# The two routing exponentials on ScalarE, issued at the end of the turn that makes the scores instead of in the next one

## The chip, the cores and the metric

The kernel is one program on one core of a Trainium2 chip. The metric is the device time of one execution in microseconds (us), as the median of several runs. The engines are named as the profile names them: PE is TensorE's matmuls and PEld its weight loads, DVE is VectorE, ACT is ScalarE, POOL is GpSimd, and SP is SyncE, which here only issues DMAs.

## What is computed

Two layers over x (16 batches of 256 tokens, width 256), float32 throughout, matrix products in split high and low parts. Each layer is attention followed by a feed-forward part:

```python
x = x + L0_xattn(ctx, layernorm(x))      # stage A of the kernel
x = x + L0_ffn(layernorm(x))             # gelu, low-rank extra weights per batch
x = x + L1_xattn(layernorm(x), ctx, ctx)
x = x + L1_ffn(layernorm(x))             # 8 experts, routed
```

The change is in the last line's routing, of which this is the part that matters:

```python
inh = sigmoid(x @ Wr / temperature)
in_zone = (inh >= GOLDEN_LOWER) & (inh <= GOLDEN_UPPER)
dist = abs(inh - GOLDEN_CENTER)
w = exp(-dist / 0.1) * in_zone
fb = exp(-dist / 0.3)
...                     # top 2 of fb where w is empty, then both normalised
out = einsum('bte,betd->btd', weights, e_out)   # e_out of all 8 experts
```

## The kernel before

Stage A (names with a_) runs the first attention and writes x1 to HBM. Stage B (names with b_), from about 1150 us on, does the rest: one turn for each batch. Turn t holds the dense part of batch t (the gelu layer, the second attention, the routing scores) and, woven into it, the experts of batch t - 1. There are 17 turns, t = 0 to 16: turn 0 has no experts, turns 1 to 14 are the hardware loop, turn 15 has no next batch, and turn 16 has experts only. A turn has eight slots, e = 0 to 7. Each engine has its own in-order list of instructions, written out by hand slot by slot, and the engines meet at counting semaphores only.

In slot e of a turn, PE makes gate and up of expert e + 1 (`gate_up`, into b_ps_g and b_ps_u) and then the down product of expert e (`down`, into b_ps_d), with the dense pieces, called fills, between: H are the gelu layer's columns, Y its second product, K, V, Q, S, T, O the attention, A, B, C the transposes behind a layer norm, R the routing scores. `gate_up` of expert 0 of batch t stands in slot 7 of turn t, `gate_up` of expert 1 in slot 0 of turn t + 1.

ACT turns a gate into `silu` (L998, b_act_e), and copies the hidden product into its high part (`hidden_high`, L1002, b_heh). DVE multiplies by up (`hidden`, L1167), makes the low part (`hidden_low`, L1171, b_hel) and adds the weighted down product to acc (`weigh`, L1184). `weights_high` (L990) and `weights_low` (L1147) split pieces of the gelu layer's weights, which POOL has summed with a low-rank term (`low_rank`, L923 and L933) in b_stage.

The scores of batch t are fill R of slot 6: ACT takes a tanh (L1040), DVE makes b_dist from it (L1233 to L1240) and signals `dist_ready`. The two exponentials are `routing_exps`. DVE's `routing` (L1265 to L1303) makes the weights b_wts from them in 14 small steps, in four parts within slot 0 of the next turn. In that slot DVE's order is: `hidden` of expert 1, routing part 0, `hidden_low` of expert 1, part 1, low part of fill H0, part 2, low part of H1, part 3 and b_wts, one `weights_low`, `weigh` of expert 0. What comes after depends on it so:

```python
def weigh(i, e):
    dve.wait_ge(down_full, i * E + e + 1)
    if e == 0:
        dve.wait_ge(wts_ready, i + 1)
...
def down(i, e):
    pe.wait_ge(he_lo, i * E + e + 1)
    pe.wait_ge(acc_ready, i * E + e + 1)     # weigh of expert e - 1
```

An ACT function that is not in the set of tables at hand needs an ACT_TABLE_LOAD; the build puts it ahead of the function, where ACT's order asks for it. Silu and tanh share one set here, gelu has another, exp a third; the plain copy is in all.

Of the kernel before, what the change touches and what calls it, by code (L numbers as in the profile page):

```python
# [632 lines left out]
def ffn_attention_experts(nc, x1, ctxT, out, lora, W1T, b1, W2T, b2, scale, WqT, bq, WkT, bk, WvT, bv, Wg, Wu, Wd, Wr,  # L633
# [5 lines left out]
    E = Wg.shape[0]  # L639
# [10 lines left out]
    def slot(e, nb, nn):  # L650
        if e == 0 and nb:
            return [("H", n) for n in range(HC // 2)], []
        if e == 1 and nb:
            return [], [("Y",)]
        if e == 2 and nb:
            return [("K",), ("V",)], [("B",)]
        if e == 3 and nb:
            return [("Q",)], [("S",)]
        if e == 4 and nb:
            return [("T",)] + ([("A",)] if nn else []), [("O",)]  # L660
        if e == 5 and nb:
            return [], [("C",)]
        if e == 6 and nb:
            return [], [("R",)]
        return [], []

    def turn_fills(nb, nn):
        return [f for e in range(E) for part in slot(e, nb, nn) for f in part]
# [19 lines left out]
    with ctx:  # L688
# [74 lines left out]
        def sections_of(eng, body):  # L763


            first = Fills(names_all, 1, 1, start)
            body(first, 0, False, True, True)
            with eng.Fori(1, B - 1) as t:
                body(Fills(names_all, 1, 1, first, F, FH, t), t, True, True, True)
            loop = Fills(names_all, 0, 0, None)  # L770
            last = Fills(turn_fills(True, False), 1 + F * (B - 1), 1 + FH * (B - 1), loop)
            body(last, B - 1, True, True, False)
            body(Fills([], 0, 0, last), B, True, False, False)
# [27 lines left out]
        def warm_pieces(e):  # L801
            first = 3 + sum(WARM_SLOTS[:e])
            return range(first, first + sum(WARM_SLOTS[e:e + 1]))
# [169 lines left out]
        def _(act):  # L973
            def warm_high(k):
                act.wait_ge(weights.loaded[k // 3], 3 * 16)
                raw, dh, _ = warm_weight(k)
                nc.scalar.activation(dh, raw, ACT.Copy, scale=QSCALE if k == 0 else 1.0).then_inc(warm_hi, 1)
# [5 lines left out]
            def weights_high(n, k):  # L983

                act.wait_ge(stage_sum, n * CHUNKS + k + 1)
                if k < NL:
                    dst = w1h[:, k // 2, k % 2 * 2 * D:(k % 2 + 1) * 2 * D]
                else:
                    dst = w2h[:, 2 * (k - NL):2 * (k - NL) + 2, :].rearrange("p c d -> p (c d)")
                nc.scalar.activation(dst, stage[:, k % STAGES, :], ACT.Copy).then_inc(stage_hi, 1)  # L990

            def context_high(t):
                act.wait_ge(ct_in, t * 16 + 16)
                nc.scalar.activation(cth[:], ct_raw[:], ACT.Copy).then_inc(ct_hi, 1)

            def silu(i, e):
                act.wait_ge(gate_full, i * E + e + 1)
                nc.scalar.activation(act_e[:, e % 2, :], ps_g[:], ACT.Silu).then_inc(silu_done, 1)  # L998

            def hidden_high(i, e):  # L1000
                act.wait_ge(he_ready, i * E + e + 1)
                nc.scalar.activation(heh[:, e % 2].rearrange("p c s -> p (c s)"), act_e[:, e % 2, :], ACT.Copy)\  # L1002
                    .then_inc(he_hi, 1)
# [45 lines left out]
            def routing_exps(t):  # L1049
                act.wait_ge(dist_ready, t + 1)  # L1050
                nc.scalar.activation(wz[:], dist[:], ACT.Exp, scale=-1.0 / 0.1).then_inc(exps_ready, 1)
                nc.scalar.activation(fb[:], dist[:], ACT.Exp, scale=-1.0 / 0.3).then_inc(exps_ready, 1)
# [9 lines left out]
            def turn(fills, t, experts, nb, nn):  # L1062
                i = 0

                def highs(names):
                    nonlocal i
                    for _ in names:
                        high(fills, i, t, experts)
                        i += 1

                def steps_of(e, part):
                    for k in PIECES.get((e, part), ()) if nn else ():
                        weights_high(t + 1, k)
                    for k in (LATE if experts else LATE_FIRST).get((e, part), ()) if nb else ():
                        weights_high(t, k)

                for e in range(E):
                    steps_of(e, 0)
                    if e + 1 < E and experts:
                        silu(t - 1, e + 1)  # L1080
                    elif e + 1 == E and nb:
                        silu(t, 0)
                    before, after = slot(e, nb, nn)
                    if e == 0 and experts:
                        routing_exps(t - 1)
                        hidden_high(t - 1, 1)
                    highs(before[:2])
                    if not experts:
                        for k in warm_pieces(e):
                            warm_high(k)  # L1090
                    if e == 1 and nb:
                        context_high(t)
                    if 0 < e < E - 1 and experts:
                        hidden_high(t - 1, e + 1)
                    elif e + 1 == E and nb:
                        hidden_high(t, 0)
                    steps_of(e, 1)
                    highs(before[2:])
                    highs(after)
                    steps_of(e, 2)  # L1100
            sections_of(act, turn)

        @block.vector
# [474 lines left out]
```

## Time and profile before

| | |
|---|---|
| time, 3 runs | 2188.25 us median, 2186.59 to 2188.69 |
| the profiled execution: span | 2184.7 us |
| PE busy | 91% |
| DVE busy | 71% |
| ACT busy | 52% |
| POOL busy | 29% |
| mean granted clock of TensorE | 0.967 |

The profiled execution is known by its span from the first to the last instruction, 2184.7 us; the median of the runs is 3.55 us above it, a difference of 0.2% that holds what lies around the span and the scatter of the runs. Busy shares are means over stages with different limits, so they don't say what a wait in one slot is worth. A clock of 1.00 is TensorE at 2.4 GHz, 0.5 is 1.2 GHz.

### The profile page before, as it was taken

To read this page: it belongs to the slowest core of one execution; us is meant where nothing else is said; L and a number is where in the kernel's file an instruction comes from. 1 tells how busy PE (TensorE), PEld (TensorE's weight loads), DVE (VectorE), ACT (ScalarE), POOL (GpSimd) and SP (SyncE) were. 2 spreads that over 40 slices of the span, in tenths; PEclk is the share of its full clock that TensorE was granted. 3 is DMA by queue.
4 is the path that set the end of the run, shared out by engine and by line. 5 is a ranking of instruction groups with operands and counts; after the bars stand their busy time and mean duration, and the time that the engine had idled before them with its cause. 6 is when DMAs were issued, how large, how long until landed. Compare 5 with 4: busy or idle time off the path is not lost.

```text
span 2184.7 us, 43173 instructions
## 1 busy us (share of the span) xinstructions
PE 1993.4 (91%) x14080; PEld 1855.1 (85%) x14080; DVE 1540.9 (71%) x3506; ACT 1133.3 (52%) x2307; POOL 636.3 (29%) x802
## 2 busy tenths in 40 slices
PE   6999999999999999999458889889889988889988
PEld 5888888888888888888348889888889888889888
DVE  6777767676767777776466787777776777786765
ACT  5565555565555556555254554455454455454442
POOL 1222222222222222221223444234444234443220
PEclk9999999999999999999768999999999999999999
DMA  5000000000000000000231222111222111212100
GB/s 176 11 20 19 19 19 10 10 19 19 19 19 19 10 10 19 19 10 10 78 101 35 73 66 69 53 63 38 72 63 72 53 63 38 72 63 72 53 20 11
DMA packets 86022, 92.16 MB, mean 42 GB/s; under 512 B 7008, under 2 KB 77024, under 8 KB 85984
## 3 DMA queue, kind: packets, MB, share of 16 engines
q1 hardware_dynamic: 82720, 88.53, 13.1%
q10 hardware_dynamic: 3264, 3.15, 0.4%
q8 instruction: 21, 0.34, 0.1%
q14 instruction: 17, 0.14, 0.0%
HBM read 83.00 MB, written 8.65 MB: 42 GB/s over the span
## 4 chain that ended last, share of the span: by engine, by line
PE 17%; DVE 16%; issue 9%; DMA 3%; ACT 3%; DVEq 1%; SPq 1%; POOL 0%; ACTq 0%; POOLq 0%
DMA b_even<-lora_rows 3%; PE b_ring L1401 3%; PE b_ring L1402 3%; PE b_ring L1403 3%; DVE b_acc L1184 3%; DVE b_act_e L1167 1%; ACT b_heh L1002 1%; PE b_ps_d L1401 1%; DVE b_w1l L1147 1%; PE b_ps_d L1403 1%; PE b_ps_d L1402 1%; PE b_ps_g L1401 1%; PE b_ps_g L1403 1%; PE b_ps_g L1402 1%; PE b_ps_u L1401 1%
## 5 line engine op out<-in xcount | busy, mean ns | idle before, releaser
L236 POOL TENSOR_SCALAR a_pr<-a_pr,a_rinv 128x512 f32<-128x512 f32 x256 | 182.4, 726 | 489.0 <-DVE a_rinv L441 486.1
L317 ACT ACTIVATE a_pr<-a_sim,a_nmax 128x512 f32<-128x512 f32 x256 | 174.3, 688 | 201.5 <-DVE a_nmax L431 201.5
L1401 PE MATMUL b_ps_d<-b_weh,b_heh 128*128 128x256 f32 x512 | 154.2, 301 | 62.2 <-DVE b_acc L1184 62.2
L998 ACT ACTIVATE b_act_e<-b_ps_g 128x512 f32<-128x512 f32 x128 | 76.3, 596 | 187.5 <-PE b_ps_g L1403 187.0
L499 PE MATMUL a_ring<-a_kvh,a_weights_low 128*128 128x512 f32 (+1 forms) x512 | 172.0, 336 | 0.0
L408 DVE SCALAR_TENSOR_TENSOR a_ktl<-a_ring,a_bkv_s,a_kth 128x512 fp32r<-128x512 f32 x128 | 95.2, 744 | 102.0 <-ACT a_kth L296 102.0
L422 DVE TENSOR_TENSOR a_ptl<-a_ring,a_pth 128x512 fp32r<-128x512 f32 x256 | 163.7, 681 | 1.2
L431 DVE TENSOR_REDUCE a_nmax<-a_sim 128x1 f32<-128x512 f32 x256 | 163.5, 679 | 0.3 <-PE a_sim L499 0.3
L1401 PEld LDWEIGHTS b_ps_d<-b_weh,b_heh 128*128 128x128 f32 x512 | 103.4, 202 | 65.2 <-issue 63.3
L898 POOL TENSOR_SCALAR b_rows<-b_mv 128x2 f32<-128x2 f32 x48 | 9.6, 199 | 508.9 <-DVE b_mv L1116 508.9
L1002 ACT ACTIVATE b_heh<-b_act_e 128x512 fp32r<-128x512 f32 x128 | 80.9, 632 | 144.4 <-DVE b_act_e L1167 144.4
L1403 PE MATMUL b_ps_d<-b_weh,b_hel 128*128 128x256 f32 x512 | 152.0, 297 | 0.0
L418 DVE TENSOR_TENSOR a_vl<-a_ring,a_vh 128x512 fp32r<-128x512 f32 x128 | 88.5, 692 | 89.3 <-ACT a_vh L304 89.3
L933 POOL TENSOR_TENSOR b_stage<-b_stage,b_ln 128x512 f32<-128x512 f32 x96 | 136.7, 1424 | 45.2 <-DVE b_stage L1136 30.9
L1401 PE MATMUL b_ps_g<-b_xch,b_weh 128*128 128x256 f32 x512 | 148.6, 290 | 0.0
L497 PE MATMUL a_ring<-a_pth,a_vh 128*128 128x256 f32 x512 | 144.5, 282 | 3.5 <-DVE a_ptl L422 3.4
L1402 PE MATMUL b_ps_g<-b_xcl,b_weh 128*128 128x256 f32 x512 | 144.9, 283 | 0.0
L499 PE MATMUL a_ring<-a_pth,a_vl 128*128 128x256 f32 x512 | 144.8, 283 | 0.0
L498 PE MATMUL a_ring<-a_ptl,a_vh 128*128 128x256 f32 x512 | 144.8, 283 | 0.0
L1401 PE MATMUL b_ps_u<-b_xch,b_weh 128*128 128x256 f32 x512 | 144.5, 282 | 0.0
L1402 PE MATMUL b_ps_u<-b_xcl,b_weh 128*128 128x256 f32 x512 | 144.2, 282 | 0.0
L307 ACT ACTIVATE a_pth<-a_ring 128x512 fp32r<-128x512 f32 x256 | 139.2, 602 | 0.0
(224 smaller groups left out, 7345.0 us busy)
## 6 DMA issues: line engine op xcount, KB each, us to landing
b_stage<-in_W1T SPq DMA_DIRECT2D x64, 256.0 KB, 2.9
b_even<-lora_rows SPq DMA_DIRECT2D x32, 512.0 KB, 5.9
b_stage<-in_W2T SPq DMA_DIRECT2D x64, 256.0 KB, 2.7
a_c_in<-in_ctx_in SPq DMA_DIRECT2D x16, 256.0 KB, 2.8
a_x_in<-in_x SPq DMA_DIRECT2D x16, 256.0 KB, 3.0
a_x_res<-in_x SPq DMA_DIRECT2D x16, 256.0 KB, 2.8
x_between<-a_x_out SPq DMA_DIRECT2D x16, 256.0 KB, 2.2
b_x_s<-x_between SPq DMA_DIRECT2D x16, 256.0 KB, 2.6
```

What stands on the lines that cost most here:

```text
L236: nc.gpsimd.tensor_scalar(pr[:, h % 2, t, :], pr[:, h % 2, t, :], rinv[:, h % 2, t:t + 1], 1.0, ALU.mult, ALU.mult).then_inc(prob_ready, 1)
L307: nc.scalar.activation(pth[:, :, name[2] * P:(name[2] + 1) * P], bank[:].rearrange("p (k q) -> p k q", k=KT), ACT.Copy).then_inc(ring_hi, 1)
L317: nc.scalar.activation(pr[:, h % 2, t, :], sim[t][:], ACT.Exp, bias=nmax[:, h % 2, t:t + 1], accum_out=rsum[:, h % 2, t:t + 1]).then_inc(e ...
L422: nc.vector.tensor_tensor(ptl[:, :, cols], bank[:].rearrange("p (k q) -> p k q", k=KT), f32(pth[:, :, cols]), ALU.subtract).then_inc(ring_ ...
L431: nc.vector.tensor_reduce(nmax[:, h % 2, t:t + 1], sim[t][:], AX.X, ALU.max, negate=True)\
L497: nc.tensor.matmul(out, lh, rh, start=(n == 0), stop=False)
L498: nc.tensor.matmul(out, lh, rl, start=False, stop=False)
L499: last = nc.tensor.matmul(out, ll, rh, start=False, stop=(n == len(parts) - 1))
L933: nc.gpsimd.tensor_tensor(stage[:, k % STAGES, :], stage[:, k % STAGES, :], ln[:].rearrange("p c d -> p (c d)"), ALU.add).then_inc(stage_s ...
L1401: nc.tensor.matmul(out, lh, rh, start=(n == 0), stop=False)
L1402: nc.tensor.matmul(out, lh, rl, start=False, stop=False)
L1403: last = nc.tensor.matmul(out, ll, rh, start=False, stop=(n == len(parts) - 1))
```

## The change

`routing_exps` is called in another place of ACT's list: no more in slot 0 of the turn of the experts, behind `silu` of expert 1, but at the very end of slot 7 of the turn before, for the same batch. Nothing is computed otherwise, and no other engine's list is touched.

```diff
@@ -1082,7 +1082,6 @@
                         silu(t, 0)
                     before, after = slot(e, nb, nn)
                     if e == 0 and experts:
-                        routing_exps(t - 1)
                         hidden_high(t - 1, 1)
                     highs(before[:2])
                     if not experts:
@@ -1098,6 +1097,8 @@
                     highs(before[2:])
                     highs(after)
                     steps_of(e, 2)
+                    if e + 1 == E and nb:
+                        routing_exps(t)
             sections_of(act, turn)
```

ACT's list before, where a turn of the loop ends (L768 is the loop's branch) and slot 0 of the next begins; b_act_e is silu, b_wz and b_fb are the two exponentials, b_heh is `hidden_high`:

```order
L1002 ACTIVATE b_heh<-b_act_e 128x512
L985 REGISTER_ALU
L990 ACTIVATE b_w1h<-b_stage 128x512
L768 REGISTER_ALU
L768 COMPARE_AND_BRANCH
L990 ACTIVATE b_w2h<-b_stage 128x512
L998 ACTIVATE b_act_e<-b_ps_g 128x512
L1051 ACT_TABLE_LOAD
L1051 ACTIVATE b_wz<-b_dist 128x16
L1052 ACTIVATE b_fb<-b_dist 128x16
L1002 ACTIVATE b_heh<-b_act_e 128x512
L1027 ACT_TABLE_LOAD
```

The same place in ACT's list of the change:

```order
L990 ACTIVATE b_w1h<-b_stage 128x512
L1051 ACT_TABLE_LOAD
L1051 ACTIVATE b_wz<-b_dist 128x16
L1052 ACTIVATE b_fb<-b_dist 128x16
L768 REGISTER_ALU
L768 COMPARE_AND_BRANCH
L990 ACTIVATE b_w2h<-b_stage 128x512
L998 ACT_TABLE_LOAD
L998 ACTIVATE b_act_e<-b_ps_g 128x512
L1002 ACTIVATE b_heh<-b_act_e 128x512
L1027 ACT_TABLE_LOAD
```

The exponentials and their table load stand ahead of a piece of weights and of silu of expert 1, and silu now has a table load of its own: one more in each of these turns.

The piece of the difference at the end of turn 15 and in turn 16, which has no weights to split and no gelu:

```order
 L998 ACTIVATE b_act_e<-b_ps_g 128x512
 L1002 ACTIVATE b_heh<-b_act_e 128x512
-L998 ACTIVATE b_act_e<-b_ps_g 128x512
 L1051 ACT_TABLE_LOAD
 L1051 ACTIVATE b_wz<-b_dist 128x16
 L1052 ACTIVATE b_fb<-b_dist 128x16
-L1002 ACTIVATE b_heh<-b_act_e 128x512
-L998 ACT_TABLE_LOAD
+L998 ACT_TABLE_LOAD
+L998 ACTIVATE b_act_e<-b_ps_g 128x512
+L1002 ACTIVATE b_heh<-b_act_e 128x512
 L998 ACTIVATE b_act_e<-b_ps_g 128x512
```

Here the number of table loads stays; the load for silu moves from behind to ahead of silu of expert 1.

## Rows read from the trace of the kernel before

**Rows 1.** The waits of PE, 1160 us to the end: total us, times, longest.

```profile
PE b_ps_d L1401 <- DVE b_acc L1184: 62.2, 17, 4.2
```

**Rows 2.** Timeline of PE, 1371.6 to 1372: start, us, instruction [idle before].

```profile
1371.67 0.36 PE L1401 MATMUL b_ps_d<-b_weh,b_heh 128*128 128x256 f32 x1 [3.79 <-DVE b_acc L1184]
```

**Rows 3.** Timeline of DVE, 1354 to 1372.

```profile
1358.25 0.67 DVE L1147 TENSOR_TENSOR b_w2l<-b_stage,b_w2h 128x512 fp32r<-128x512 f32 x1
1358.85 0.67 DVE L1167 TENSOR_TENSOR b_act_e<-b_act_e,b_ps_u 128x512 f32<-128x512 f32 x1
1359.44 0.67 DVE L1265 TENSOR_TENSOR b_wz<-b_wz,b_near 128x16 f32<-128x16 f32 x1
...
1364.23 0.71 DVE L1277 TENSOR_TENSOR b_fb<-b_fb,b_mask 128x16 f32<-128x16 f32 x1
...
1366.09 1.26 DVE L1280 TENSOR_SCALAR b_rows<-b_rows 128x2 f32<-128x2 f32 x1
...
1369.94 0.17 DVE L1303 TENSOR_TENSOR b_wts<-b_wz,b_rows 128x16 f32<-128x16 f32 x1
```

**Rows 4.** Timeline of ACT, 1354.5 to 1361.6.

```profile
1355.06 0.61 ACT L990 ACTIVATE b_w1h<-b_stage 128x512 fp32r<-128x512 f32 x1
1355.88 0.63 ACT L990 ACTIVATE b_w2h<-b_stage 128x512 fp32r<-128x512 f32 x1 [0.21 <-POOL b_stage L933]
1356.42 0.58 ACT L998 ACTIVATE b_act_e<-b_ps_g 128x512 f32<-128x512 f32 x1
1357.02 1.28 ACT L1051 ACT_TABLE_LOAD   x1
1358.31 0.22 ACT L1051 ACTIVATE b_wz<-b_dist 128x16 f32<-128x16 f32 x1
1358.44 0.20 ACT L1052 ACTIVATE b_fb<-b_dist 128x16 f32<-128x16 f32 x1
```

**Rows 5.** Timeline of ACT, 1399 to 1400.5.

```profile
1399.90 0.60 ACT L998 ACTIVATE b_act_e<-b_ps_g 128x512 f32<-128x512 f32 x1
```

**Rows 6.** Timeline of DVE, 1399 to 1401.6.

```profile
1400.53 0.69 DVE L1167 TENSOR_TENSOR b_act_e<-b_act_e,b_ps_u 128x512 f32<-128x512 f32 x1 [1.11 <-ACT b_act_e L998]
```

**Rows 7.** Timeline of POOL, 1354 to 1368.

```profile
1358.30 1.78 POOL L933 TENSOR_TENSOR b_stage<-b_stage,b_ln 128x512 f32<-128x512 f32 x1 [0.18 <-POOL b_ln L923]
1360.65 1.42 POOL L923 TENSOR_TENSOR b_ln<-b_even,b_odd 128x256 f32<-128x256 f32 x2 [0.56 <-POOL b_stage L933]
1362.25 1.29 POOL L933 TENSOR_TENSOR b_stage<-b_stage,b_ln 128x512 f32<-128x512 f32 x1 [0.18 <-POOL b_ln L923]
1363.72 1.90 POOL L923 TENSOR_TENSOR b_ln<-b_even,b_odd 128x256 f32<-128x256 f32 x2 [0.18 <-POOL b_stage L933]
1365.70 1.62 POOL L933 TENSOR_TENSOR b_stage<-b_stage,b_ln 128x512 f32<-128x512 f32 x1
```

**Rows 8.** Timeline of DVE, 2085.3 to 2093.2 (slot 0 of turn 15).

```profile
2087.09 1.26 DVE L1277 TENSOR_TENSOR b_fb<-b_fb,b_mask 128x16 f32<-128x16 f32 x1
...
2092.02 0.17 DVE L1303 TENSOR_TENSOR b_wts<-b_wz,b_rows 128x16 f32<-128x16 f32 x1
```

**Rows 9.** Timeline of POOL, 2081 to 2090.

```profile
2086.62 1.70 POOL L933 TENSOR_TENSOR b_stage<-b_stage,b_ln 128x512 f32<-128x512 f32 x1
```

**Rows 10.** Timeline of ACT, 2140 to 2147.6 (end of turn 15, turn 16).

```profile
2140.66 0.63 ACT L1002 ACTIVATE b_heh<-b_act_e 128x512 fp32r<-128x512 f32 x1 [1.61 <-DVE b_act_e L1167]
2142.72 0.60 ACT L998 ACTIVATE b_act_e<-b_ps_g 128x512 f32<-128x512 f32 x1 [1.43 <-PE b_ps_g L1403]
```

**Rows 11.** Timeline of DVE, 2143 to 2145.6.

```profile
2144.21 0.69 DVE L1167 TENSOR_TENSOR b_act_e<-b_act_e,b_ps_u 128x512 f32<-128x512 f32 x1 [1.41 <-PE b_ps_u L1403]
2145.09 0.18 DVE L1265 TENSOR_TENSOR b_wz<-b_wz,b_near 128x16 f32<-128x16 f32 x1 [0.20 <-ACT b_fb L1052]
```

**Rows 12.** Windows behind PE's wait: us, busy (count) of PE, PEld, DVE, ACT, POOL, clock, DMA.

```profile
1370.00:1380.00 10.00, 7.95 (x54) 7.68 (x55) 6.60 (x13) 4.79 (x8) 0.00 (x0) 0.83 0.10 26
...
1632.00:1642.00 10.00, 8.36 (x50) 8.39 (x51) 6.58 (x13) 4.77 (x8) 0.00 (x0) 0.66 0.08 26
```

## The prediction

> **What bounds the kernel now.** PE is busy for 91% of the span, so I read first what PE waits for. In the table of waits one entry stands out in stage B: `down` of expert 1 waits for `weigh` of expert 0, 62.2 us in all, the longest 4.2 us [rows 1]. The timeline of PE at one such place has 3.79 us of idle time [rows 2]. There is one such wait in each of the 16 turns with experts, in slot 0 or, in turn 16, at its head. So whatever delays `weigh` of expert 0 delays PE, one for one, and what hastens it is a gain of up to 3.79 us a turn.
>
> Behind `weigh` stands DVE's list. In its timeline DVE goes from `weights_low` (1358.25) to `hidden` of expert 1 (1358.85), the first routing step (1359.44) and on to b_wts at 1369.94 with hardly a gap [rows 3]. The second exponential has ended at 1358.44 + 0.20 = 1358.64 [rows 4]. DVE comes to the routing at 1359.44, 0.80 us later. So in the loop the exponentials are not waited for: DVE's own list sets the pace. Only in turn 16 does the first step wait for them, 0.20 us [rows 11].
>
> The third reader is POOL, whose sums run beside this until 1365.70 + 1.62 = 1367.32 [rows 7]. Several DVE steps on 16 or fewer columns, which elsewhere take 0.16 to 0.18 us, take far longer here, and end when a POOL instruction ends: the first routing step at 1360.11 (POOL 1360.08), L1280 at 1367.35 (POOL 1367.32) [rows 3, 7]. DVE and POOL shut each other out for whole instructions, so a delay on DVE need not come out at the same size.
>
> **The change, part by part.** *What it takes away.* Two exponentials and a table load leave the place between silu of expert 1 and `hidden_high` of expert 1. They ended at 1358.64, and `hidden_high` can't start before `hidden` at 1358.85 has run, so nothing was waiting: 0. In turn 16 the wait of 0.20 us goes.
>
> *What it adds ahead of silu of expert 1.* I rebuild ACT's list from its rows. The last piece of weights of the turn ends at 1355.06 + 0.61 = 1355.67. Then a table load of 1.28, to 1356.97 with the 0.02 that stands ahead of the load in the rows. Exponentials: the first starts 0.01 after its load, and the second ends 0.33 after the first starts (1358.31 to 1358.64), so to 1357.31. b_dist is long there, it came in slot 6. Then the piece b_w2h; it starts some 0.02 before the end of the second exponential and takes 0.63: to 1357.92. Then the new table load of silu, to 1359.22, and silu, 0.60, to 1359.82. Before, silu ended at 1356.42 + 0.58 = 1357.00, with 1.85 us to spare until DVE came for it at 1358.85. Now it is late. How soon DVE starts once silu has ended is to be seen in another slot: silu ends at 1400.50, `hidden` starts at 1400.53 [rows 5, 6]. So `hidden` moves from 1358.85 to 1359.86, by 1.0 us. That is the stall the change makes: 2.82 us more on ACT (1359.82 - 1357.00) less 1.85 us of slack, plus 0.03.
>
> Queued ahead on DVE, `weights_low` of the same piece starts at 1358.25 and needs b_w2h, now at 1357.92 instead of 1356.51: still in time by 0.3 us. The stage buffers that it frees, their DMAs on SP and POOL's sums are then not late. PE needs silu of expert 1 only for the gate of expert 2 and `down` 0 not at all; both were covered before and stay so. Queued behind `hidden` on DVE is the whole routing, then `weigh` of expert 0, for which PE waits.
>
> What a load itself costs is plain here: L1051's load starts at 1357.02, takes 1.28 and the exponential starts at 1358.31 [rows 4]. The Trainium skill (ScalarE: Activation LUTs, What ACT_TABLE_LOAD costs) adds a drain of about 1.38 us to each load, 2.66 us together. By that silu would be later by another 2 x 1.38 us, and 15 turns would cost some 41 us more. The trace disagrees, the next instruction starts 0.01 us behind the load, so the sum goes by 1.28.
>
> *What POOL makes of 1.0 us.* I carry the delay through the two lists. `hidden` reads PSUM and is not held up. The first routing step comes at 1360.46 instead of 1359.44: it finds POOL between two instructions (1360.08 to 1360.65) and takes 0.16, not 0.67, so half a microsecond comes back. L1270, the first step on the maxima, then comes about 1.1 us later, at 1361.6, and meets POOL's products, which end at 1360.65 + 1.42 = 1362.07, so 1362.10. L1272 comes 0.3 behind its predecessor's start, at about 1362.3, 0.07 after POOL's sum has begun (1362.25 to 1363.54): ends 1363.57. L1275 meets the products from 1363.72 on; its two steps and `hidden_low` (0.68) end at about 1365.8. POOL's last sum, waiting since 1365.3, goes then, 1.29 on its own, to about 1367.0. L1277 is queued behind it and ends at 1367.04. The same pattern is in the trace once, in turn 15: L1277 is held for 1.26 us, to 2088.35, by POOL's sum that ends at 2088.32, and b_wts starts at 2092.02, 3.70 after that end [rows 8, 9]. So here b_wts comes at 1367.0 + 3.7 = 1370.7, against 1369.94: **0.8 us** later. The bounds are 0 (POOL's last end holds L1280 in both cases) and 1.0 (no give and take), and I take 0.8 for each of the 15 turns 1 to 15: 12.0 us.
>
> *Turn 16.* No POOL. ACT is idle between `hidden_high` of expert 0 (ends 2141.29) and silu (2142.72) [rows 10]. Load, exponentials and load fill it: 2141.29 + 1.30 + 0.33 + 1.30 = 2144.22, silu to 2144.82. `hidden` starts at 2144.85, not 2144.21; the first routing step follows 0.60 later (from 1358.85 to 1359.44 in rows 3) at 2145.45 instead of 2145.09: 0.4 us.
>
> *The clock.* Behind PE's wait the granted clock falls to 1.2 GHz for a while. I read 16 windows of 10 us, each from about the end of the wait: 11 have a mean clock of 0.83, as the first row shows, 5 have 0.66, as the second [rows 12]. The difference is 0.17 x 10 = 1.7 us of PE's time. The idle time grows from 3.79 to about 4.6 us, and the longest wait of all, 4.2 us [rows 1], is followed by one of the five. Bounds: none more, or all of the other 11, 11 x 1.7 = 19 us. I take two or three more: 4 us.
>
> **The sum.** 12.0 + 0.4 + 4 = 16.4 us on a span of 2184.7, 2201.1. The median of the runs is 3.55 us above that execution's span: **2204.6 us**, +0.75%. A measurement of this kernel tells about 0.2% (4.4 us) from no change.
>
> **The rivals.**
> - *Full delay.* POOL's pattern shifts with DVE, or the order of L1272 and POOL's sum comes out so that more is held: 1.0 to 1.3 a turn, and half of the other gaps get the long stretch of slow clock (9 us): 15 x 1.15 + 0.4 + 9 = 27, 2215. For it: L1272 loses by only 0.07 us. Against: POOL's end comes earlier by my walk, not later.
> - *Swallowed.* POOL's last sum holds the chain at 1367.3 as before: if L1277 gets in ahead of that sum, L1280 is what waits for it, as now, and the 1.0 us of stall is given back by shorter holds. 15 x 0 + 0.4 and no clock, 2188.7. Against it: in the rows `hidden_low` is followed by exactly this race now (POOL's products at 1363.72, L1277 at 1364.23), and POOL wins, L1277 being held to 1364.94. The Trainium skill (SBUF — State Buffer, Who interferes with whom) says that whoever issues first has the shared port for its whole instruction; that speaks for POOL in this race too, and leaves the 0.8.
> - *Faster, the other side.* That the exponentials come early frees ACT between silu and `hidden_high`, and the routing finds its inputs. A gain needs the routing to have waited for them. If the hold of DVE's first routing step (0.67 us) was such a wait in disguise, its 0.51 over 0.16 comes back in 15 turns and the silu must arrive in time as well, that is the added 2.82 us must be under 1.85: at most 15 x 0.51 + 0.2 = 7.9, 2180.4. It decides only if the second table load doesn't occur or lies in idle time, and ACT has none there (0.21 and then none).
> - *Nothing of the stall,* since silu's load is fetched while ACT waits: 2188. ACT does not wait there in the loop.
>
> **How the numbers follow.** Forecast (0.5 to 0.9 a turn, clock 0 to 8) 66%; full delay and more 16%; swallowed, wholly or to under 4 us, 12%; faster 3%; nothing 3%. The forecast's own span is 15 x 0.5 + 0.4 = 7.9 to 15 x 0.9 + 0.4 + 8 = 21.9 above 2188.25; the range reaches into full delay on the one side and to 4.8 us above on the other, halfway to swallowed: 2193 to 2214. Faster by over 0.2% 0.03, within 0.2% 0.11, slower 0.86.
>
> **What would show it.** In the profile after: L998 has 15 more table loads; in slot 0 DVE idles about 0.9 us before L1167, released by ACT's silu; b_wts comes about 0.8 us later counted from the same piece of PE's work; PE's wait for b_acc grows from 62 to about 74 us; L1280 is short and L1277 long; and more windows at 0.66. The prediction is wrong if that wait does not grow, if `hidden` starts on time, or if the clock takes most of the difference.

## The result and the profile after

The change made the kernel slower: 2197.1 us median (2196.8 to 2198.21) against 2188.35 us for the kernel before in the same set, +8.75 us, ratio 1.0044 with a 95% interval of 1.0029 to 1.0058. The forecast was +16.4 us, 2204.6, with a range of 2193 to 2214: the time lies in the range, in its lower part, at little more than half of the forecast difference. The profiled executions have spans of 2184.7 before and 2195.2 after, 10.5 us apart. In every execution the device time is some 1.8 us above the span, so the profiled one of before ran 1.8 us below its kernel's median and the one after sits on its own (2197.0): 10.5 and 8.75 are the same difference, to what two single executions can tell.

The waits of PE after, from 1160 us to the end (total us, times, longest), then the page's group of `down`, then two rows of the answer on `silu`'s line, its table loads and who waited for silu, and the same two rows of before. Line numbers behind the change are one higher:

```profile
PE b_ps_d L1402 <- DVE b_acc L1185: 72.0, 17, 4.6
```

```profile
L1402 PE MATMUL b_ps_d<-b_weh,b_heh 128*128 128x256 f32 x512 | 153.4, 300 | 72.0 <-DVE b_acc L1185 72.0
```

```profile
L998 ACT ACT_TABLE_LOAD  x47: 1283/1283/1283, 1154.7 to 2154.0; - x47
  DVE b_act_e L1168: 32.1, 31
```

```profile
L998 ACT ACT_TABLE_LOAD  x32: 1283/1283/1283, 1153.8 to 2145.6; - x32
  DVE b_act_e L1167: 17.3, 15
```

The wait for b_acc, 62.2 us in [rows 1], is 72.0 us now, 9.8 us more, and so it stands in the page's group. Silu's line has 47 table loads where it had 32, and DVE now waits for silu 31 times, not 15: in each of the turns 1 to 16 once more. From PE's wait in turn 1 (it ends at 1175.42 before, at 1176.16 after) to its last wait (2179.59 and 2190.03) the two executions differ by 9.7 us, so from there on the wait is their whole difference.

ACT's timeline around the start of turn 4, to be held against [rows 4]. The anchor here is the last piece of weights of the turn, 1356.64 now and 1355.06 there, so the same place of the work stands 1.58 us later in this trace:

```profile
1356.64 0.62 ACT L990 ACTIVATE b_w1h<-b_stage 128x512 fp32r<-128x512 f32 x1
1357.27 1.28 ACT L1051 ACT_TABLE_LOAD   x1
...
1358.80 0.61 ACT L990 ACTIVATE b_w2h<-b_stage 128x512 fp32r<-128x512 f32 x1
1359.43 1.28 ACT L998 ACT_TABLE_LOAD   x1
1360.72 0.60 ACT L998 ACTIVATE b_act_e<-b_ps_g 128x512 f32<-128x512 f32 x1
```

Silu ends at 1361.32, which is 1359.74 in the times of before; the prediction had 1359.82. Nothing stands between a load and its neighbours but 0.01 to 0.02 us. DVE and POOL in the same place, to be held against [rows 3] and [rows 7]:

```profile
1359.82 0.68 DVE L1148 TENSOR_TENSOR b_w2l<-b_stage,b_w2h 128x512 fp32r<-128x512 f32 x1
1361.35 0.69 DVE L1168 TENSOR_TENSOR b_act_e<-b_act_e,b_ps_u 128x512 f32<-128x512 f32 x1 [0.86 <-ACT b_act_e L998]
1361.96 0.17 DVE L1266 TENSOR_TENSOR b_wz<-b_wz,b_near 128x16 f32<-128x16 f32 x1
...
1363.88 1.25 DVE L1273 TENSOR_SCALAR b_rows<-b_rows 128x2 f32<-128x2 f32 x1
...
1367.28 1.26 DVE L1278 TENSOR_TENSOR b_fb<-b_fb,b_mask 128x16 f32<-128x16 f32 x1
...
1369.49 0.16 DVE L1281 TENSOR_SCALAR b_rows<-b_rows 128x2 f32<-128x2 f32 x1
...
1372.24 0.17 DVE L1304 TENSOR_TENSOR b_wts<-b_wz,b_rows 128x16 f32<-128x16 f32 x1
```

```profile
1359.88 1.77 POOL L933 TENSOR_TENSOR b_stage<-b_stage,b_ln 128x512 f32<-128x512 f32 x1 [0.18 <-POOL b_ln L923]
1362.22 1.42 POOL L923 TENSOR_TENSOR b_ln<-b_even,b_odd 128x256 f32<-128x256 f32 x2 [0.56 <-POOL b_stage L933]
1363.82 1.29 POOL L933 TENSOR_TENSOR b_stage<-b_stage,b_ln 128x512 f32<-128x512 f32 x1 [0.18 <-POOL b_ln L923]
1365.29 1.44 POOL L923 TENSOR_TENSOR b_ln<-b_even,b_odd 128x256 f32<-128x256 f32 x2 [0.18 <-POOL b_stage L933]
1366.81 1.69 POOL L933 TENSOR_TENSOR b_stage<-b_stage,b_ln 128x512 f32<-128x512 f32 x1
```

```profile
1373.97 0.55 PE L1402 MATMUL b_ps_d<-b_weh,b_heh 128*128 128x256 f32 x1 [4.52 <-DVE b_acc L1185]
```

DVE idles 0.86 us for silu. The first routing step then takes 0.17 us, not 0.67: it finds POOL between two instructions (1361.65 to 1362.22). The step on the row sums (L1273) is held for 1.25 us, and ends at 1365.13 with POOL's sum (1365.11). L1278, L1277 before, is held for 1.26 us, until 1368.54 (POOL 1368.50), and L1281, L1280 before, is free, 0.16 instead of 1.26. b_wts starts at 1372.24, that is 1370.66 in the times of before, against 1369.94 in [rows 3]: 0.72 us later. PE's idle time is 4.52 against 3.79 in [rows 2].

All of turns 2 to 14 look like this one, with idle times of 4.49 to 4.57 us. Three turns differ. In turn 1 and in turn 15 PE's wait has not grown: in turn 15 it is 4.18 us, where the longest of before was that turn's 4.2 [rows 1]. POOL's holds there gave the whole delay back. For turn 15 the rows say how: its L1277 was held by POOL's last sum in the kernel before already, for 1.26 us [rows 8, 9], and L1278 is held for 1.26 us now, so the end of that sum sets b_wts in both:

```profile
2099.11 1.26 DVE L1278 TENSOR_TENSOR b_fb<-b_fb,b_mask 128x16 f32<-128x16 f32 x1
```

In turn 16 the wait has grown by 0.4 us: `hidden` waits for silu, and the first step comes that much later than it did behind its own wait for the exponentials [rows 11]. 13 x 0.72 + 0.4 = 9.8 us, which is the growth of the wait.

The granted clock made no difference between these two executions in stage B (their means over everything, 0.967 and 0.969, differ by stage A, 0.97 and 0.98). Of the 16 windows of 10 us behind the waits, 9 have a mean of 0.83, 6 have 0.66 and one, turn 1's, has 1.00:

```profile
1174.00:1184.00 10.00, 7.19 (x58) 7.01 (x59) 6.84 (x14) 5.20 (x9) 0.00 (x0) 1.00 0.11 27
1241.00:1251.00 10.00, 8.58 (x58) 8.47 (x59) 6.36 (x12) 4.49 (x7) 0.00 (x0) 0.83 0.10 26
...
1372.00:1382.00 10.00, 8.03 (x47) 8.06 (x48) 6.76 (x14) 5.02 (x8) 0.00 (x0) 0.66 0.08 26
```

By the price of [rows 12] that is 9 x 1.7 + 6 x 3.4 = 35.7 us of PE's time against 11 x 1.7 + 5 x 3.4 = 35.7 before: one more long stretch, one short one less.

This price is too high, and that changes what the clock can explain below. It takes all time at the low clock to be time in which PE works at half its speed. The length of a turn, from one b_wts to the next, shows what arrives. In the kernel before, the turns from turn 2 to turn 14 last 66.2 us on average where the stretch behind the wait is a long one (a window of 0.66; 3 turns) and 65.5 us where it is a short one (0.83; 9 turns); after the change 67.0 us (5 turns) and 66.0 us (7 turns). In these two traces a long stretch costs 0.7 to 0.9 us more than a short one, not 1.7.

### The profile page after: what moved, and what is told of

The parts are those of the page before. It is cut to its first block, busy times and chain, and to the rows that moved or that the text cites. A ratio compares the mean times of both kernels' runs of the same rounds, so it can differ in the third digit from the quotient of the medians.

```text
span 2195.2 us, 43188 instructions
## 1 busy us (share of the span) xinstructions
PE 1992.6 (91%) x14080; PEld 1854.0 (84%) x14080; DVE 1537.3 (70%) x3506; ACT 1151.9 (52%) x2322; POOL 629.3 (29%) x802
## 4 chain that ended last, share of the span: by engine, by line
PE 17%; DVE 15%; issue 9%; ACT 5%; DMA 3%; DVEq 1%; POOL 0%; SPq 0%; ACTq 0%; POOLq 0%
PE b_ring L1402 3%; DMA b_even<-lora_rows 3%; PE b_ring L1404 3%; PE b_ring L1403 3%; DVE b_acc L1185 2%; DVE b_act_e L1168 1%; ACT L998 1%; PE b_ps_d L1402 1%; PE b_ps_d L1404 1%; PE b_ps_d L1403 1%; DVE b_w1l L1148 1%; ACT b_heh L1002 1%; PE b_ps_g L1402 1%; PE b_ps_g L1404 1%; PE b_ps_g L1403 1%
## 5 line engine op out<-in xcount | busy, mean ns | idle before, releaser
L1168 DVE TENSOR_TENSOR b_act_e<-b_act_e,b_ps_u 128x512 f32<-128x512 f32 x128 | 87.3, 682 | 79.3 <-PE b_ps_u L1404 47.2
```

Of the source, the lines that this page charges most:

```text
L1168: nc.vector.tensor_tensor(act_e[:, e % 2, :], act_e[:, e % 2, :], ps_u[:], ALU.mult).then_inc(he_ready, 1)
```

## The experiments

Theory: silu of expert 1 comes too late behind a table load, the exponentials and a second load, and the mutual holds of DVE and POOL decide what of it reaches PE. The rivals are that an added table load, or the place, costs by itself, and that the clock makes the difference. Each ratio is to the kernel before, timed in the same set: 2186.39 us for e0, e1, e2 and e5, and 2186.22 us on another chip for e3, e4, e6 and e7.

**The change once more, as a control (e0_after).** No edit.

> The changed kernel once more, as the control of this set. Theory (silu of expert 1 comes 0.94 us too late, of which DVE's list passes on 0.72 us a turn): as measured first, +8 to +10 us, PE's wait for b_acc 72 us in all, that is 4.5 us in each of turns 2 to 14. Rival (most of the difference is the slow clock, which falls otherwise from run to run): the difference to the kernel before moves by more than 3 us, and the number of long stretches of slow clock behind the waits is no longer near 6 of 16.

Measured: 2195.7 us (2193.74 to 2200.99) against 2186.39, ratio 1.0053 (1.0041 to 1.0065), that is +9.3 us, as the theory said. The wait for b_acc is 72.0 us again and turns 2 to 14 have 4.49 to 4.54 us each. The windows behind the waits have 7 of the long slow stretches (0.66) and 9 short ones, against 6 and 9 in the first execution. So the wait is the same to the tenth. By the price of 1.7 us the clock costs 9 x 1.7 + 7 x 3.4 = 39.1 us here, 3.4 more, and yet this execution has the shorter span, 2193.2 against 2195.2 us; PE's wait for b_ln, 9.4 us there, is 6.6 us here. The single executions of this set spread over 7 us. The rival of the clock isn't borne out: the difference to the kernel before is the same and so is the wait.

**The exponentials further ahead still (e1_exps_behind_silu0).**

```diff
                     elif e + 1 == E and nb:
                         silu(t, 0)
+                        routing_exps(t)
...
                     if e == 0 and experts:
-                        routing_exps(t - 1)
                         hidden_high(t - 1, 1)
```

> The exponentials move further ahead still, right behind silu of expert 0 in slot 7, where ACT idles for about 3 us before hidden_high of expert 0. As many table loads as in the change. Theory (the loss is the table load and exponentials between the last piece of weights and silu of expert 1): only silu's own load, 1.30 us, is left there, under the 1.85 us of slack, so hidden of expert 1 is on time: 2188, 0 to -1 us against before, PE's wait 3.8 us a turn. Rival (an added table load costs its time wherever it stands, or early exponentials as such cost): +8 us or more.

Measured: 2183.46 us (2179.73 to 2189.62), ratio 0.9992 (0.9984 to 1.0001); no difference. ACT's timeline at the end of turn 3 and the start of turn 4:

```profile
1349.38 0.60 ACT L998 ACTIVATE b_act_e<-b_ps_g 128x512 f32<-128x512 f32 x1 [0.65 <-PE b_ps_g L1403]
1350.00 1.28 ACT L1051 ACT_TABLE_LOAD   x1
1351.87 0.22 ACT L1051 ACTIVATE b_wz<-b_dist 128x16 f32<-128x16 f32 x1 [0.59 <-DVE b_dist L1240]
...
1355.09 1.28 ACT L998 ACT_TABLE_LOAD   x1
1356.39 0.60 ACT L998 ACTIVATE b_act_e<-b_ps_g 128x512 f32<-128x512 f32 x1
```

DVE's `hidden` of that turn:

```profile
1357.40 0.67 DVE L1167 TENSOR_TENSOR b_act_e<-b_act_e,b_ps_u 128x512 f32<-128x512 f32 x1
```

That is as the theory said, within the noise. The load and the exponentials fit into ACT's idle time ahead of `hidden_high` of expert 0, and even wait there for b_dist, 0.59 us. Silu ends at 1356.99, 0.41 us before DVE asks for it. There are as many table loads as in the change, and no loss: the added load is free where ACT idles. The waits for b_acc are 62.1 us, as before.

**The place of the change without the loads (e2_copies_no_loads).**

```diff
-nc.scalar.activation(wz[:], dist[:], ACT.Exp, scale=-1.0 / 0.1).then_inc(exps_ready, 1)
-nc.scalar.activation(fb[:], dist[:], ACT.Exp, scale=-1.0 / 0.3).then_inc(exps_ready, 1)
+nc.scalar.activation(wz[:], dist[:], ACT.Copy, scale=-1.0 / 0.1).then_inc(exps_ready, 1)
+nc.scalar.activation(fb[:], dist[:], ACT.Copy, scale=-1.0 / 0.3).then_inc(exps_ready, 1)
```

> The place of the change, but both exponentials are plain copies with a scale, which need no table load: this leaves the exponentials of the routing out (the routing weights are other numbers, all instructions on the other engines are the same). Theory: 0.33 us more ahead of silu of expert 1 and no load, inside the slack of 1.85 us: 2188, within 1 us of before. Rival (the place as such costs, by the wait for b_dist or by the two instructions at the loop's branch): +8 us.

Measured: 2185.24 us (2182.07 to 2189.33), ratio 0.9999 (0.999 to 1.0007). The waits for b_acc are 61.8 us in all and 3.76 to 3.83 in turns 2 to 14. The place as such costs nothing.

**The same place, plain copies instead of the loads (e6_copies_and_padding).** As e2, and behind the second copy:

```diff
+for n in range(4):
+    nc.scalar.activation(hh[:, 2 * n:2 * n + 2, :], wqkvh[:, 0], ACT.Copy)
+for n in range(2):
+    nc.scalar.activation(gel[0][:, n * D:(n + 1) * D], wqkvh[:, 0, 0, :], ACT.Copy)
```

> As e2_copies_no_loads (the exponentials of the routing left out, copies in their place, no table load), with six plain copies more behind them, 2.8 us on ACT into tiles that nobody reads then. Silu of expert 1 ends about as late as in the change. Theory (the loss is lateness of silu alone, whatever fills the time): hidden of expert 1 about 0.9 us later, PE's wait 4.5 us in turns 2 to 14, +7 to +10 us, as the change. Rival (the table loads cost by themselves): like e2_copies_no_loads, 2185 to 2188, with waits of 3.8 us.

Measured: 2197.42 us (2195.11 to 2202.8), ratio 1.0053 (1.0038 to 1.0068), as the change. Its waits, and DVE's timeline at the start of turn 4:

```profile
PE b_ps_d L1406 <- DVE b_acc L1189: 72.1, 17, 4.5
```

```profile
1364.23 1.03 DVE L1152 TENSOR_TENSOR b_w2l<-b_stage,b_w2h 128x512 fp32r<-128x512 f32 x1 [0.81 <-ACT b_w2h L990]
1365.19 0.67 DVE L1172 TENSOR_TENSOR b_act_e<-b_act_e,b_ps_u 128x512 f32<-128x512 f32 x1
...
1367.00 1.21 DVE L1275 TENSOR_SCALAR b_rows<-b_rows 128x2 f32<-128x2 f32 x1 [0.16 <-DVE b_top_at L1274]
```

A table load isn't needed for the loss; time on ACT does it, though not quite by the way expected. The copies come ahead of the piece b_w2h, and here DVE waits for that piece (0.81 us) before it comes to `hidden`; silu, behind the piece, is there by then. So `hidden` is 1.25 us late and not 0.9. Counted from the end of PE's up product of expert 1 (1356.48 in the kernel before, so 1358.85 - 1356.48 = 2.37 for `hidden`), `hidden` starts at 3.62 us against 2.37 in the kernel before and 3.30 in the change, but b_wts at 14.16 against 13.46 and 14.19. So a delay of 1.25 us and one of 0.93 us both come out as 0.7. What reaches b_wts is set by where POOL's instructions end, not by the size of the delay.

**The same pair without POOL beside it (e3_before_quiet_pool, e4_after_quiet_pool).** Both kernels with this edit in `low_rank`:

```diff
+if k >= CHUNKS - 3:
+    last = nc.gpsimd.memset(ln[:, 0, 0:8], 0.0)
-for c in range(DC):
+for c in range(DC) if k < CHUNKS - 3 else ():
...
+w = 2 * D if k < CHUNKS - 3 else 8
-nc.gpsimd.tensor_tensor(stage[:, k % STAGES, :], stage[:, k % STAGES, :], ...
+nc.gpsimd.tensor_tensor(stage[:, k % STAGES, 0:w], stage[:, k % STAGES, 0:w], ...
```

> The kernel before, with POOL's work on weight pieces 5, 6 and 7 cut to 8 columns: this leaves most of the low-rank term of these pieces out. All waits and the lists of the other engines stay. It is the pair of e4_after_quiet_pool and read against it. Theory (DVE's and POOL's holds pass on only a part of the delay): DVE's routing steps all take 0.16 to 0.23 us, hidden of expert 1 comes about 0.5 us earlier than in the kernel before, b_wts some 7 us after hidden instead of 11.1, and PE's wait of 3.8 us all but goes: below 2120 us.

> The changed kernel with the same cut on POOL; it leaves the same out. Silu of expert 1 then comes at its time of the change, and the distance between the two kernels of this pair in hidden of expert 1 is 1.4 to 1.5 us. Theory (what was given back, 0.94 us on hidden and only 0.72 on b_wts, was given back by POOL's holds): without POOL there is nothing to give back, b_wts is later by the whole of hidden's delay, within 0.1 us, and the pair differs by 10 us or more. Rival (DVE's list has a fixed slack of 0.2 us behind hidden, whatever POOL does): b_wts is later by 0.2 us less than hidden, or more if gelu on ACT is what DVE waits for.

Measured: 2110.04 us (ratio 0.9654, 0.9639 to 0.967) and 2133.89 us (0.9763, 0.9746 to 0.978), 23.9 us apart. DVE in turn 4 without the change, then with it:

```profile
1341.23 0.68 DVE L1170 TENSOR_TENSOR b_act_e<-b_act_e,b_ps_u 128x512 f32<-128x512 f32 x1
1341.82 0.17 DVE L1268 TENSOR_TENSOR b_wz<-b_wz,b_near 128x16 f32<-128x16 f32 x1
...
1348.79 0.18 DVE L1306 TENSOR_TENSOR b_wts<-b_wz,b_rows 128x16 f32<-128x16 f32 x1
```

```profile
1349.90 0.69 DVE L1171 TENSOR_TENSOR b_act_e<-b_act_e,b_ps_u 128x512 f32<-128x512 f32 x1 [1.22 <-ACT b_act_e L1001]
1350.51 0.17 DVE L1269 TENSOR_TENSOR b_wz<-b_wz,b_near 128x16 f32<-128x16 f32 x1
...
1357.47 0.17 DVE L1307 TENSOR_TENSOR b_wts<-b_wz,b_rows 128x16 f32<-128x16 f32 x1
```

From `hidden` to b_wts there are 7.56 us without and 7.57 us with the change, where they were 11.09 and 10.89 with POOL at work. From the end of up, `hidden` goes from 1.84 to 3.30 and b_wts from 9.40 to 10.87: 1.46 and 1.47 us. The whole delay arrives, nothing is given back, so the 0.2 us that were given back in the real kernel were POOL's. In turns 2 to 14 PE's wait for b_acc is at most 0.29 us without the change and 1.70 to 1.73 us with it; in all it is 9.8 and 32.5 us, which is nearly all of the difference of the two. The rival of a fixed slack is out.

**The early place used (e5_early_and_first_steps).** As e1, and on DVE:

```diff
-first, last = ((0, 5), (5, 7), (7, 11), (11, ROUTE))[part]
+first, last = ((2, 5), (5, 7), (7, 11), (11, ROUTE), (0, 2))[part]
...
                     elif e + 1 == E and nb:
+                        routing(t, 4)
                         hidden_low(t, 0)
```

with the wait for the exponentials in part 4.

> As e1_exps_behind_silu0, and the first two of the 14 routing steps on DVE move from slot 0 to slot 7 of the turn before, between hidden and hidden_low of expert 0, where DVE idles 0.70 us for ACT. Theory: with the exponentials done at about 1353.7 the two steps (1.0 us of instructions, 0.7 of it in the idle time) leave the list ahead of weigh, so b_wts comes 0.6 to 1.2 us earlier a turn and PE's wait falls to about 3.0: -9 us, 2179 (0.996). Rival (POOL holds the steps up in their new place, or hands the hold on to the next step): nothing gained, 2188, with the waits at 3.8.

Measured: 2169.4 us (2168.14 to 2173.03), ratio 0.9926 (0.9914 to 0.9939): faster than both kernels, and by 17 us, not 9. Its waits, PE's timeline in turn 4, and the window behind that wait:

```profile
PE b_ps_d L1402 <- DVE b_acc L1184: 51.3, 17, 3.4
PE b_ring L1402 <- DVE b_w1l L1147: 16.3, 14, 1.2
```

```profile
1371.51 0.36 PE L1402 MATMUL b_ps_d<-b_weh,b_heh 128*128 128x256 f32 x1 [3.09 <-DVE b_acc L1184]
```

```profile
1371.00:1381.00 10.00, 9.45 (x65) 9.18 (x66) 5.80 (x11) 3.58 (x6) 0.00 (x0) 0.83 0.08 26
```

The wait for b_acc falls by 62.2 - 51.3 = 10.9 us, a little more than the expected 9. The clock, which the expectation left out, has improved as well: 1 window of 16 has 0.66, 14 have 0.83 and one 1.00. By the price of 1.7 us that is 14 x 1.7 + 3.4 = 27.2 against 35.7 us, 8.5 us less, and 10.9 + 8.5 = 19.4 us. The profiled executions differ by 2184.7 - 2171.2 = 13.5 us, so of these 8.5 us some 2.6 arrive. The medians differ by 17 us; the profiled execution is the slowest of its five.

**More steps early (e7_first_five_steps).** As e5, with the parts `((5, 5), (5, 7), (7, 11), (11, ROUTE), (0, 5))`.

> As e5_early_and_first_steps, with the first five routing steps in slot 7 instead of two. Theory (the idle time of DVE there is 0.70 us and is used up): three more steps, 2 to 3 us with POOL's holds, push weights_low ahead of fill H0, so PE's wait for b_w1l grows by about what its wait for b_acc falls: the sum of the two about as in e5_early_and_first_steps, 2166 to 2176. Rival (more steps early are more gain): another 1.5 us a turn, 2150.

Measured: 2187.61 us (2186.56 to 2190.57), ratio 1.0012 (1.0004 to 1.0021).

```profile
PE b_ring L1402 <- DVE b_w1l L1147: 61.0, 14, 4.5
...
PE b_ps_d L1402 <- DVE b_acc L1184: 5.9, 8, 1.7
```

```profile
1757.00:1767.00 10.00, 8.50 (x49) 8.51 (x50) 8.71 (x17) 6.31 (x12) 6.56 (x6) 0.66 0.27 79
```

The wait has moved nearly whole, from b_acc to b_w1l, and the sum of the two, 66.9 us, is that of e5 (67.6), as the theory said. The time is neither what the theory said (2166 to 2176) nor the rival's 2150: it is 18 us more than in e5, and 13.6 us between the two profiled executions (2171.2 and 2184.8). Of these, 6.5 us are waits of PE: all its waits in stage B are 90.9 us in e5 and 97.4 here, mostly by the wait for b_w2l, 0.6 us there and 7.1 here. One wait of 4.5 us has taken the place of two of 1.2 and 3.1, and 9 of the 16 windows behind it have 0.66 to 0.74 where e5 has one. That the clock took the rest isn't shown: between b_wts of turn 2 and of turn 14, turns with a long stretch last 65.8 us here (8 turns) and those with a short one 65.9 (4 turns), where all of e5's, with short ones, last 64.9. What the other 7 us are stays open.

## Why the prediction was right, step by step

- *PE waits for `weigh` of expert 0, one for one.* Right. The wait is 9.8 us longer; the span is 10.5 us longer, 9.7 of it behind PE's wait in turn 1.
- *Nothing waits for the exponentials, so taking them away gains 0.* Right; e1 has them 5 us earlier at no gain. Their wait in turn 16 went, 0.2 us, as said.
- *ACT's list: 2.82 us more, 1.85 us of slack, `hidden` 1.0 us later.* Measured 0.93 from the same point of PE's work. The piece b_w2h starts at once behind the exponentials, with 0.09 us of overlap where I had 0.02. That lateness is the cause, and not the load or the place, is shown by e1, e2 and e6 together.
- *POOL gives back 0.2 us: 0.8 a turn.* Right in its mechanism and almost in its size: L1277 held by the last sum, L1280 free, b_wts 3.7 us behind POOL's end, 0.72 us. It was applied to all of turns 1 to 15; in turns 1 and 15, where POOL runs at another phase, the delay was given back whole. For turn 15 that could be read ahead: I took its rows as the pattern of what the change would do, so it had that pattern already and nothing was to come on top. 13 x 0.72 + 0.4 = 9.8 instead of 15 x 0.8 + 0.4 = 12.4: this term was 2.6 us too large.
- *The clock, 4 us.* This is the term that was most mis-sized. The direction was right: the profiles have 1 long stretch in 16 at a wait of 3.1 us (e5), 5, 3 and 4 at 3.8 us (before, e1, e2), 6, 7 and 8 at 4.5 us (the change, e0, e6). That is three more on average, and I took two or three, but from one case, the longest wait. The profile of before, with 5, was the highest of its kind and that of after, with 6, the lowest, so between these two nothing came of it. The price of 1.7 us was wrong: a long stretch adds 0.7 to 0.9 us to its turn in these two traces. And the times leave little for it: the three kernels with waits of 4.5 us are 8.75, 9.3 and 11.2 us slower than the kernel before, and their waits are 9.8 to 9.9 us longer.
- *The scale.* The sum was put on top of a median that lay 1.8 us above the profiled execution's own time, and the difference of the medians was 8.75, not 10.5.
- *The sum.* The path was right and the size of the wait right to 2.6 us. The 16.4 us are nearly twice the 8.75 measured by these 2.6 us, the clock's 4 us and 1.8 us of scatter, less the 0.7 us that the spans differ beyond the wait. The time still fell into the range, 4 us above its lower end; the range was wide enough for that, and the point forecast was not close.
- *The rivals.* Full delay (27 us) would have needed POOL out of step with DVE. Swallowed came true in two turns of sixteen, in one of them because the pattern was there before. A gain by the exponentials being early didn't occur.

## What to carry to other kernels

An instruction that is moved ahead to where "nobody waits for it" is moved past its neighbours: ask which of them gets late, and count the slack of that one, here 1.85 us against 2.82. With function tables, a move can split two functions of one set and add a load; the load is free only in time in which the engine idles, and such a place, 3 us wide, lay a few instructions further ahead in the same slot (e1). An early result is worth something only once its consumer is moved as well; then the pair gave 0.7% (e5). It stops there as soon as the consumer fills the idle time of its own engine and pushes something else back (e7).

## What the runs showed of the hardware beyond what was expected

DVE and POOL, shutting each other out for whole instructions, pass a delay on in steps: 0.93 us and 1.25 us on `hidden` both became 0.7 us on b_wts, and in two turns nothing. The same holds make the routing chain 11.09 us long; it is 7.56 us with POOL's last three pieces cut to 8 columns. That kernel takes 3.5% less time, but it leaves most of POOL's work on these pieces out, so this is no gain that could be had by avoiding the holds alone.

The longer PE's wait, the more of the slow stretches behind it are long: 1 of 16 at waits of 3.1 us, 3 to 5 at 3.8 us, 6 to 8 at 4.5 us. A long one is 1.7 us of the clock's time more than a short one, but only 0.7 to 0.9 us of a turn's, before and after the change. Counting windows by their mean clock gave more time than arrived: 19.4 us for the 13.5 of e5.
